# A two-layer graph network on one core: the order of work in the first batch and in its passage to the second

## The reference

```
h = relu(layernorm(x))
Xw = h @ Wv + bv;  sj = Xw @ aw[:256];  si = Xw @ aw[256:]
e = leaky_relu(sj[None, :] + si[:, None] + ab, 0.2)
alpha = adj * exp(e);  T = alpha / (alpha.sum(-1) + 1e-12)
H = h @ Wk[0] + (T h) @ Wk[1] + (T T h) @ Wk[2] + bk[0] + bk[1] + bk[2]
x = x + relu(H)
h = relu(layernorm(x));  Ah = adj + I;  dh = rsqrt(Ah.sum(-1))
out = x + relu((dh * Ah * dh.T) @ h @ kernel + bias)
```

## Time and profile before

| | before |
|---|---|
| median of 3 runs | 758.02 us |
| profiled execution, own time | 757.64 us |
| its span | 755.8 us |
| granted TensorE clock, mean | 0.999 |
| busy PE / PEld / DVE / ACT / POOL | 745.3 / 686.2 / 624.5 / 536.8 / 187.2 us |

### The profile page before, as it was taken

How to read it: one execution, slowest core, us unless ns; L and a number is a source line. 1 busy time by engine, 2 the same in 40 slices (tenths; PEclk the granted TensorE clock), 3 DMA queues, 4 the chain that set the end, 5 groups by cost and what they waited for, 6 DMA issues and landing times.

```text
span 755.8 us, 14028 instructions
## 1 busy us (share of the span) xinstructions
PE 745.3 (99%) x5099; PEld 686.2 (91%) x5099; DVE 624.5 (83%) x1414; ACT 536.8 (71%) x1047; POOL 187.2 (25%) x193
## 2 busy tenths in 40 slices
PE   8899999999999999999999999999999999999997
PEld 8688988989899897999979999899988999889986
DVE  7898798878888789877989878897888877986665
ACT  3898795668955789567885679766696667956352
POOL 3031240322403133130322214122150312402331
PEclk9999999999999999999999999999999999999999
DMA  7576548734587255762568635776358654555521
GB/s 227 210 250 232 143 159 296 245 123 155 177 283 249 87 186 191 263 225 89 190 200 284 225 90 178 240 248 224 103 159 275 215 205 134 160 189 173 161 87 56
DMA packets 63909, 143.32 MB, mean 190 GB/s; under 512 B 6768, under 2 KB 32864, under 8 KB 63840
## 3 DMA queue, kind: packets, MB, share of 16 engines
q1 hardware_dynamic: 55072, 111.75, 45.4%
q10 hardware_dynamic: 8768, 30.68, 11.9%
HBM read 133.96 MB, written 8.45 MB: 188 GB/s over the span
## 4 chain that ended last, share of the span: by engine, by line
PE 94%; DVE 4%; issue 1%; DMA 1%; ACT 0%; POOL 0%; POOLq 0%; DVEq 0%; ACTq 0%
PE acc L1220 15%; PE acc L1222 15%; PE acc L1221 15%; PE da L1084 14%; PE db L1084 8%; PE da L1185 4%; PE tp L1185 4%; PE tp L1187 4%; PE da L1187 4%; PE da L1186 4%; PE tp L1186 4%; DVE t_raw L840 1%; PE acc L1116 1%; DVE t_lo L845 1%; DMA tg_a<-adj_t_dram 1%
## 5 line engine op out<-in xcount | busy, mean ns | idle before, releaser
L1220 PE MATMUL acc<-g_hi,t_hi 128*128 128x256 f32 (+1 forms) x976 | 276.6, 283 | 0.1
L1222 PE MATMUL acc<-g_hi,t_lo 128*128 128x256 f32 (+1 forms) x976 | 275.2, 282 | 0.0
L1221 PE MATMUL acc<-g_lo,t_hi 128*128 128x256 f32 x976 | 274.6, 281 | 0.0
L1220 PEld LDWEIGHTS acc<-g_hi,t_hi 128*128 128x128 f32 x976 | 183.8, 188 | 0.9 <-DVE g_lo L814 0.3
L1221 PEld LDWEIGHTS acc<-g_lo,t_hi 128*128 128x128 f32 x976 | 184.3, 189 | 0.3
L1222 PEld LDWEIGHTS acc<-g_hi,t_lo 128*128 128x128 f32 x976 | 184.1, 189 | 0.0
L423 POOL TENSOR_TENSOR g_lo<-tmp,g_hi 128x256 fp32r<-128x256 f32 x64 | 59.8, 935 | 263.9 <-ACT g_hi L608 263.9
L851 DVE TENSOR_TENSOR a_lo<-a_raw,a_hi 128x512 fp32r<-128x512 f32 x128 | 93.9, 748 | 24.1 <-ACT a_hi L596 24.1
L553 ACT ACTIVATE tg_e<-si,sij 128x256 f32<-128x256 f32 x256 | 109.2, 499 | 0.1
L596 ACT CAST a_hi<-a_raw 128x512 fp32r<-128x512 f32 x128 | 76.7, 616 | 26.4 <-DVE a_raw L891 17.9
L429 POOL TENSOR_TENSOR hs_lo<-tmp,hs_hi 128x256 fp32r<-128x256 f32 x64 | 59.8, 955 | 89.3 <-ACT hs_hi L493 89.3
(11 more groups left out here) (201 smaller groups left out, 1608.6 us busy)
## 6 DMA issues: line engine op xcount, KB each, us to landing
a_raw<-adj_dram SPq DMA_DIRECT2D x64, 512.0 KB, 4.4
a_raw<-adj_z_dram SPq DMA_DIRECT2D x64, 512.0 KB, 4.6
tg_a<-adj_t_dram ACTq DMA_DIRECT2D x58, 512.0 KB, 4.2
x_o<-x_dram SPq DMA_DIRECT2D x64, 128.0 KB, 3.4
out_dram<-x_o SPq DMA_DIRECT2D x58, 128.0 KB, 4.1
x_nat<-x_dram SPq DMA_DIRECT2D x28, 256.0 KB, 4.6
xt<-x_t_dram SPq DMA_DIRECT2D x28, 256.0 KB, 5.5
si<-mean_rows_dram SPq DMA_DIRECT2D x7, 512.0 KB, 4.6
```

The source lines that it names most:

```text
L1220: nc.tensor.matmul(acc[:, s, 0:n], l_hi, r_hi, start=(jt == 0), stop=False)
L1221: nc.tensor.matmul(acc[:, s, 0:D], l_hi, r_lo, start=False, stop=False)
L1222: ins = nc.tensor.matmul(acc[:, s, 0:n], l_lo, r_hi, start=False, stop=(jt == NT - 1))
```

## The change

In batch 0 and in the passage to batch 1: DVE norms the first two groups of tiles before the second half of the statistics is aggregated, and adds the score constants earlier; POOL sums the three biases (`bk_sum`), which DVE did; the fill of 16 and 10 transposes becomes 4 and 5; PE turns the first score rows before the last two pairs; half of the `p0` additions go into the first dense stage; ACT rounds T between leaky-relu and exponent; one unit more is multiplied ahead of the U phase. In the passage, DVE centres two groups of the next input earlier and takes the eighth `u_chunk` after the next batch's first dense tile; three row sums stay in the U phase and five go behind tiles 0 to 4 of the dense stage (before: five and three); diagonal and layer-1 rounding move from tiles 1 to 4 to tiles 5 and 6. Batches 1 to 7 keep their order otherwise.

```diff
-    FIRST_LEAKY_D, FIRST_EXP_D, FIRST_HIGH_D = {0: 1, 4: 2, 6: 3}, {1: 1, 5: 2, 7: 3}, {2: 0, 3: 1}
-    FIRST_PROD_D, FIRST_LOW_D = {2: 1, 6: 2}, {4: 0, 5: 1}
-    FIRST_HIGH_U, FIRST_PROD_U, FIRST_LOW_U = {0: 6, 1: 7}, {0: 5, 1: 6, 2: 7}, {0: 4, 1: 5, 2: 6, 3: 7}
+    FIRST_LEAKY_D, FIRST_EXP_D, FIRST_HIGH_D = {2: 2, 6: 3}, {0: 1, 5: 2, 7: 3}, {1: 0, 3: 1}
+    FIRST_PROD_D, FIRST_LOW_D = {1: 1, 6: 2}, {2: 0, 4: 1}
+    FIRST_HIGH_U, FIRST_PROD_U, FIRST_LOW_U = {1: 7}, {0: 6, 1: 7}, {0: 5, 1: 6, 2: 7}
     FIRST_P0 = (2, 3, 0, 1, 4, 5, 6, 7)
-    FIRST_ROWS_U, FIRST_ROWS_D = {2: (0,), 3: (1,), 4: (2,), 5: (3,), 6: (4,)}, {0: (5,), 1: (6,), 3: (7,)}
+    FIRST_ROWS_U, FIRST_ROWS_D = {2: (0, 1), 4: (2,)}, {0: (3,), 1: (4,), 2: (5,), 3: (6,), 4: (7,)}
...
-    WARM = (24, 16, 10)
+    WARM = (24, 4, 5)
...
+            pool.wait_ge(loaded_w, 16 * 4)
+            nc.gpsimd.tensor_tensor(bk_sum[:, :], bk_raw[:, 0, :], bk_raw[:, 1, :], ALU.add).then_inc(bk_ready, 1)
+            pool.wait_ge(bk_ready, 1)
+            nc.gpsimd.tensor_tensor(bk_sum[:, :], bk_sum[:, :], bk_raw[:, 2, :], ALU.add).then_inc(bk_ready, 1)
...
+                    rounding = {4: 0, 6: 1} if b == 0 else {NT - 2: 0, NT - 1: 1}
+                    if i in rounding and not last:
+                        centred_hi(rounding[i], b + 1)
+                    if i == NT - 1 and b == 0:
+                        break
+                    if i > 0 or b > 0:
+                        g1_high(b, i)
                     if i == 0:
                         leaky(b, NU - 1)
+                        if b == 0:
+                            t_high(0, NU - 2, False)
                         exponent(b, NU - 1)
+                        if b == 0:
+                            g1_high(0, 0)
                     high = FIRST_HIGH_U if b == 0 else HIGH_U
                     if i in high:
                         t_high(b, high[i], last)
                     for t in (FIRST_ROWS_U if b == 0 else ROWS_U).get(i, ()):
...
                 def after(t):
+                    if t == 0 and b == 0:
+                        g1_high(0, NT - 1)
                     for r in (FIRST_ROWS_D if b == 0 else ROWS_D).get(t, ()):
                         rows(b, r)
-                    if t == 2:
+                    if t == (5 if b == 0 else 2):
                         a_round(b, 0, 0)
-                    if t == 3:
+                    if t == (6 if b == 0 else 3):
...
             first_hi(3)
-            nc.scalar.copy(wl_hi[:, :, :], wk_raw[:, 3]).then_inc(weights_rounded, 1)
             first_si_copy(0)
             leaky(0, 0)
-            first_si_copy(1)
             exponent(0, 0)
+            leaky(0, 1)
             for t in range(NT):
                 dense0(0, t)
+                if t == 2:
+                    nc.scalar.copy(wl_hi[:, :, :], wk_raw[:, 3]).then_inc(weights_rounded, 1)
+                if t == 4:
+                    first_si_copy(1)
                 if t in FIRST_LEAKY_D:
...
+                t_high(0, u - 1, False)
                 exponent(0, u)
-                t_high(0, u - 1, False)
...
+                    if t == 0 and b == 1:
+                        u_chunk(0, NT - 1)
+                        centre(2, b)
...
+                    if i in low and b == 0:
+                        t_low(b, low[i])
                     if i in prod:
                         t_prod(b, prod[i])
-                    if i in low:
+                    if i in low and b > 0:
                         t_low(b, low[i])
+                    if i == 3 and b == 0:
+                        centre(0, 1)
+                    if i == 4 and b == 0:
+                        centred_lo(0, 1)
+                    if i == 5 and b == 0:
+                        centre(1, 1)
...
-                    if t == 1:
+                    if t == (5 if b == 0 else 1):
                         diag(b, 0)
-                    if t == 3:
+                    if t == (6 if b == 0 else 3):
                         a_low(b, 0, 0)
-                    if t == 4:
+                    if t == (6 if b == 0 else 4):
...
+                if h == 1:
+                    dve.wait_ge(rstd_first, 1)
+                    norm0(0)
+                    norm0(1)
...
-            dve.wait_ge(rstd_first, 1)
-            norm0(0)
-            norm0(1)
+            then(nc.vector.tensor_tensor(cst[:, 2:3], v_s[:, KD, 0:1], v_s[:, KD, 1:2], ALU.add))
+            then(nc.vector.tensor_tensor(cst[:, 0:1], cst[:, 2:3], ab_s, ALU.add))
             dve.wait_ge(weights_rounded, 1)
             nc.vector.tensor_tensor(wb_lo[:, :, 0:D], wk_raw[:, 0], wb_hi[:, :, 0:D].bitcast(F32),
                                     ALU.subtract).then_inc(v_cols_ready, 1)
             first_lo(0)
             dve.wait_ge(rstd_first, 2)
             norm0(2)
-            then(nc.vector.tensor_tensor(cst[:, 2:3], v_s[:, KD, 0:1], v_s[:, KD, 1:2], ALU.add))
-            then(nc.vector.tensor_tensor(cst[:, 0:1], cst[:, 2:3], ab_s, ALU.add))
             first_lo(1)
             norm0(3)
             first_sij(0)
...
             first_lo(2)
             first_sij(2)
             first_sij(3)
-            dve.wait_ge(loaded_w, 16 * 4)
-            then(nc.vector.tensor_tensor(bk_sum[:, :], bk_raw[:, 0, :], bk_raw[:, 1, :], ALU.add))
-            then(nc.vector.tensor_tensor(bk_sum[:, :], bk_sum[:, :], bk_raw[:, 2, :], ALU.add))
+            first_lo(3)
+            dve.wait_ge(bk_ready, 2)
             first_p0(FIRST_P0[0])
-            first_lo(3)
             first_p0(FIRST_P0[1])
             for t in range(4, NT):
                 first_sij(t)
             first_p0(FIRST_P0[2])
-            for t in FIRST_P0[3:]:
-                first_p0(t)
+            first_p0(FIRST_P0[3])
             t_prod(0, 0)
             for t in range(NT):
                 dve.wait_ge(g2_hi_done, t + 1)
                 nc.vector.tensor_copy(p1[:, t, :], da[:, t % 2, 0:D])
                 g2_low(0, t)
+                if t < HJ:
+                    first_p0(FIRST_P0[HJ + t])
...
+            t_prod(0, 3)
+            t_low(0, 2)
+            t_low(0, 3)
+            t_prod(0, 4)
             stats0_of(1, NT - 2)
             stats0_of(1, NT - 1)
             moments0(1)
+            t_low(0, 4)
+            t_prod(0, 5)
...
-                    pe.wait_ge(g1_tmp_ready, FB)
+                    pe.wait_ge(g1_tmp_ready, FB - 1)
+                        if b == 1 and t == 1:
+                            pe.wait_ge(g1_tmp_ready, FB)
...
+            first_si(0)
             first_pair(2)
-            first_si(0)
```

More of the change, by code:

```diff
@@ L184, in gnn_two_layers @@
         v_cols_ready = sem("v_cols_ready")
+        bk_ready = sem("bk_ready")
         sij0_ready = sem("sij0_ready")
@@ L596, in a_round, with g1_high @@
                 nc.scalar.copy(a_half(a_hi, i, h), a_raw[:, i % RS, h * N // 2:(h + 1) * N // 2]).then_inc(a_hi_done[h], 1)
+            def g1_high(b, i):
+                act.wait_ge(g1_tmp_ready, b * NT + i + 1)
+                nc.scalar.copy(g1_hi[:, i, :], tmp[:, i % 2, :]).then_inc(g1_hi_done, 1)
             def batch(b, par, last):
@@ L603, in batch @@
                         mean_copy(b + 1)
-                    if i >= NT - 2 and not last:
-                        centred_hi(i - (NT - 2), b + 1)
-                    act.wait_ge(g1_tmp_ready, b * NT + i + 1)
-                    nc.scalar.copy(g1_hi[:, i, :], tmp[:, i % 2, :]).then_inc(g1_hi_done, 1)
+                    rounding = {4: 0, 6: 1} if b == 0 else {NT - 2: 0, NT - 1: 1}
[5 more added lines that the diff above has]
+                        g1_high(b, i)
                     if i == 0:
                         leaky(b, NU - 1)
+                        if b == 0:
+                            t_high(0, NU - 2, False)
                         exponent(b, NU - 1)
+                        if b == 0:
+                            g1_high(0, 0)
                     high = FIRST_HIGH_U if b == 0 else HIGH_U
@@ L924, in batch @@
                         zt_low(b - 1, 1)
+                    if i == NT - 1 and b == 0:
+                        centred_lo(1, 1)
+                        break
                     if i == NT - 1 and not last:
@@ L932, in batch @@
                             moments0(b + 1)
-                    if i in (NT - 3, NT - 2) and not last:
+                    if i in (NT - 3, NT - 2) and b > 0 and not last:
                         centre(i - (NT - 3), b + 1)
```

9 lines of the change are left out of this document (3 added, 6 removed).

## The result

| | median, us | runs | span of the profiled execution, us |
|---|---|---|---|
| before | 758.02 | 11 | 755.8 |
| changed | 760.5 | 11 | 758.8 |

The ratio is 1.0029, with a 95% interval from 1.0020 to 1.0039: the changed kernel is 0.3% slower. The time lies 0.3 us above the predicted range, and 2.0 us above the predicted time. One of the 11 runs of the changed kernel, 798.93 us at a mean clock of 0.851, was in a slower state and is left out of the ratio.

The account below looks back on a forecast made before the run. PE was taken as the bound, busy 99% of the span. An entry 2.7 us earlier becomes 0.4 us of delay in the passage, plus 0.1 for `xt` waits: 757.6 + 0.5 = 758.1, median 758.5, range 756.6 to 760.2.

Parts of the forecast that it names:

- Start: First pair of products: starts 0 to 0.4 us later (0.1 taken), at 11.9 to 12.3; 2.1 us of fill become idle.
- bias sum: First dense stage: POOL takes DVE's 1.57 us, norms beside it slow by up to 0.5; net 0.4 us earlier.
- Rival C: Start: shorter fill lets PE's clock fall back, 12 products cost 1.4 us more; end 759.5 to 760.5; chance 0.08.
- U phase: Before the second dense stage: entry at 58.7, 2.7 us earlier, bounds 58.1 and 60.5, without the `ht_lo` wait.
- Rival B: U phase: POOL's `g1_lo` and T's last units lock each other; entry at 60, end 759.9; chance 0.17.
- Passage up to the row sums: Second dense stage: ACT waits for the eighth `u_chunk`, then works serially; row sum 8 at 72.5, 0.4 us later.
- Rival A: Passage keeps pace with PE; row sum 8 is 1.3 to 1.9 us earlier, end 756.1 to 756.7; chance 0.17.
- The step that failed: Score row through DRAM: 5.8 us from issue to batch 1's first score instruction, which comes at 79.7.
- +0.1 for waits of `xt` in between: Between batch 1's scores and the `a_lo` pair: waits for x tiles add 0.1 us to the shift.
- The rest of the chain: Layer 1: PE has no reserve at `a_lo`, waits over 1 us in sum; the whole shift reaches the end, +0.5.

Follow-up runs that it names:

- start_only: The kernel before with only the changed kernel's start (fill, norm order, first score rows, GpSimd bias sum, half the `p0` additions): 758.04 us, ratio 1.0000.

## Why the prediction was wrong

- **Start, bias sum: right.** First pair at 11.86 (11.9 to 12.3 given), the clock did not fall, the group of norms beside GpSimd took 1.15 us against 0.73, and start_only is at 1.0000. Rival C is out for the changed kernel.
- **U phase: right in kind, short in size.** Entry at 58.02, not 58.7 and just under the lower bound of 58.1, and no wait for `ht_lo`. Rival B is out: the loss did not come from a late entry.
- **Passage up to the row sums: right.** ScalarE idle for 1.33 us ahead of the eighth cast, TensorE waiting 1.2 us for `g_lo`, row sum 8 at 72.47 (72.5), the row stored at 73.89 (73.9). Rival A is out.
- **The step that failed:** "from there to the first score instruction of batch 1 at 79.29 are 5.81: DMA to DRAM and back. So 72.5 + 1.4 + 5.8 = 79.7". The 5.8 was carried over as a constant. It was measured in a kernel where the DMA engines stood nearly still for 1.5 us, up to a microsecond ahead of the store; the change issues the same loads bunched in front of it. In the two executions of the changed kernel it measured 7.30 and 7.31. ScalarE itself was free at 79.6, as forecast, and stood waiting for the row. These rows (busy times by engine with their counts, clock, DMA share, GB/s) are of before and of the changed kernel, 71.0 to 72.5 us:

```profile
71.00:72.50 1.50, 1.50 (x12) 1.34 (x11) 1.43 (x3) 1.50 (x5) 0.00 (x0) 1.00 0.01 5
```

```profile
71.00:72.50 1.50, 1.50 (x11) 1.36 (x10) 0.67 (x3) 1.50 (x5) 0.00 (x0) 1.00 0.62 145
```

  The forecast looked at the row sum that releases the last `adj_z` load, and not at how far apart the four were issued: at 61.99, 65.06, 67.34 and 72.16 before, at 66.40, 68.16, 70.67 and 72.57 after.
- **A second term was missing:** the x wait, 0.75 and 0.61. "+0.1 for waits of `xt` in between" was the only allowance for the stretch from the scores to `a_lo`.
- **The rest of the chain held:** no reserve at `a_lo`, TensorE waiting there for 1.8 us in sum (over 1 was given), the shift going to the end. It is why 1.49 + 0.75 us of DRAM reached the time nearly whole.
- **The edits can't be costed one by one:** start and exponent part +1.7 us (nearly all of it the low clock behind a standstill that only this combination has), passage +3.7, both +2.4. The sum came out right for ScalarE only since the whole was followed in one chain.

## What to carry to other kernels

When a change moves the work that releases loads, list the loads again with their new issue times, and look for a small transfer that a chain waits for: its latency belongs to the schedule around it and is not a constant of the row. Such a transfer wants no large load issued shortly ahead of it or right behind it. When one half of a change is run by itself, look at the granted clock before putting its loss down to the edit: here the half made a standstill that neither whole kernel has. And before giving up an edit that loses, ask which wait took its gain: here SyncE's order alone took 0.3% slower back to no change, and with the diagonals and one cast moved as well it became 0.36% faster.
